# A recurrent layer with FP4 products on one core: the convolution over both input halves at once, and later `down` products

## The reference

```
k  = real(sum over n of W[h,n] * exp(dt[h]*Lambda[n]*l)),  l < 128    # one filter of 128 taps per feature
s  = causal convolution of xn with k along the sequence + xn * D
q(v) = v rounded to FP4 (E2M1) with one scale per 16 values, as float
h  = silu(q(xn) @ q(w_gate).T) * (q(xn) @ q(w_up).T)                   # 704 wide
g  = silu(q(h) @ q(w_down).T)
out = x + s * g
```

## Time and profile before

| | us |
|---|---|
| median of three runs | 711.54 (710.3 to 713.05) |
| the profiled execution | 711.99 |
| its span | 710.2 |
| TensorE busy (products) | 550.3 (77%) |
| VectorE busy | 587.8 (83%) |
| ScalarE busy | 404.3 (57%) |
| GpSimd busy | 193.6 (27%) |
| granted TensorE clock, mean | 0.95 |

### The profile page before, as it was taken

How to read it: one execution, slowest core, us unless ns; L and a number is a source line. 1 busy time by engine, 2 the same in 40 slices (tenths; PEclk the granted TensorE clock), 3 DMA queues, 4 the chain that set the end, 5 groups by cost and what they waited for, 6 DMA issues and landing times.

```text
span 710.2 us, 13747 instructions
## 1 busy us (share of the span) xinstructions
PE 550.3 (77%) x4856; PEld 391.6 (55%) x4856; DVE 587.8 (83%) x698; ACT 404.3 (57%) x562; POOL 193.6 (27%) x293
## 2 busy tenths in 40 slices
PE   0000087666888889999999999999999976868896
PEld 0000055234555557777777767777777744545564
DVE  7999999696998887888777758777777795979797
ACT  7940586465877765555555555555555534545554
POOL 1339410321232221111110102222111166565330
PEclk9999996888999999999999999999999997999999
DMA  6930000001000114444444444444444169674314
GB/s 208 348 105 0 0 15 16 15 4 35 16 16 16 44 44 135 132 124 128 120 138 123 125 114 135 134 128 133 127 124 129 47 114 209 152 177 85 93 59 121
DMA packets 109218, 70.79 MB, mean 100 GB/s; under 512 B 9072, under 2 KB 108912, under 8 KB 109168
## 3 DMA queue, kind: packets, MB, share of 16 engines
q1 hardware_dynamic: 101776, 62.73, 30.0%
q0 software_dynamic: 7392, 7.34, 6.9%
HBM read 61.28 MB, written 8.78 MB: 99 GB/s over the span
## 4 chain that ended last, share of the span: by engine, by line
PE 51%; DVE 11%; issue 8%; POOL 5%; DMA 3%; ACT 3%; DVEq 0%; ACTq 0%; POOLq 0%
PE ps L1208 23%; PE ps L1226 7%; PE ps L1245 6%; PE ps L1241 6%; PE ps L1228 4%; PE ps L1217 4%; DMA gbuf<-L_attn_u 3%; DVE work L851 2%; DVE work L846 2%; DVE work L877 1%; POOL gbuf L511 1%; PE ps L1196 1%; DVE xh L769 1%; ACT work L628 1%; DVE sm L793 1%
## 5 line engine op out<-in xcount | busy, mean ns | idle before, releaser
L1208 PE MATMUL ps<-wgu,work 128*128 128x512 f16 (+1 forms) x1152 | 253.7, 377 | 24.7 <-DVE work L877 23.5
L1208 PEld LDWEIGHTS ps<-wgu,work 128*128 128x128 f16 x1152 | 113.6, 101 | 142.6 <-issue 37.7
L614 ACT ACTIVATE work<-ps,con 128x704 f32<-128x704 f32 x64 | 54.2, 848 | 127.5 <-PE ps L1208 127.5
L1226 PE MATMUL ps<-wdh,work 128*128 128x256 f16 x704 | 92.4, 282 | 27.2 <-ACT work L609 27.2
L877 DVE TENSOR_TENSOR work<-work,ps 128x704 f32<-128x704 f32 x64 | 56.6, 885 | 64.8 <-ACT work L614 64.7
L609 ACT COPY work<-ps 128x1408 f16<-128x1408 f16 x64 | 84.9, 1328 | 15.5 <-PE ps L1217 15.1
L1226 PEld LDWEIGHTS ps<-wdh,work 128*128 128x128 f16 x704 | 68.5, 101 | 44.0 <-ACT work L609 32.1
L1245 PE MATMUL ps<-xh,work 128*128 x768 | 91.9, 239 | 0.0
L1241 PE MATMUL ps<-xh,work 128*128 x768 | 91.3, 238 | 0.0
L846 DVE SCALAR_TENSOR_TENSOR work<-work 128x960 f32<-128x960 bf16 (+2 forms) x67 | 71.9, 1112 | 23.3 <-ACT work L628 23.3
L511 POOL TENSOR_TENSOR gbuf<-gbuf,xh 128x512 f32<-128x512 f32 x28 | 39.9, 1450 | 126.8 <-DVE work L859 110.6
(11 more groups left out here) (152 smaller groups left out, 755.6 us busy)
## 6 DMA issues: line engine op xcount, KB each, us to landing
work<-kpad SPq DMA_DIRECT2D x64, 512.0 KB, 4.4
gbuf<-u_rev SPq DMA_DIRECT2D x4, 2048.0 KB, 18.3
work<-L_attn_u SPq DMA_DIRECT2D x32, 256.0 KB, 4.3
gbuf<-L_attn_u POOLq DMA_DIRECT2D x14, 512.0 KB, 5.9
out<-gbuf SPq DMA_DIRECT2D x14, 512.0 KB, 4.2
work<-L_attn_u SPq DMA_DIRECT2D x2, 512.0 KB, 3.7
work<-L_ffn_w_down SPq DMA_DIRECT2D x1, 704.0 KB, 7.1
work<-L_ffn_w_gate SPq DMA_DIRECT2D x1, 640.0 KB, 4.5
```

What stands on the lines that cost most here:

```text
L1208: last = T.matmul(p_gu[:, a:b], xT[par][:, t, c, :], wgu[:, part, c % 2, a:b], start=(n == 0), stop=(n == len(todo) - 1))
L1226: T.matmul(dst, hT[t][:, c, :], wdh[:, c, :], start=(c == 0), stop=False)
```

## The change

- The convolution takes both parts of `xh` as one operand of 128 columns (high tiles, then low tiles), with the template's high and low part: two products of 128 columns and two of 112 for each channel, four where there were six. (Low by low is now computed too.) The sums of the two halves come out apart: a bank holds 4 channels x 128, so a call of `conv` fills it, and each call waits for the evacuation of the one before.
- `y_copy` takes the high half to `yv` and the low half to a new buffer `ylo`, 256 values each, four calls a step; GpSimd adds them (`y_sum`, 512 values per partition, twice a step). `gated` and the tail wait for these sums (`y_p`) and not for the copies.
- The room for `ylo` is from `xhl`, which has one buffer where it had two; `x_parts` waits for the last transpose (`x_tp`). At the start `x_parts(1)` stands behind the weights. The final input `fin[1]` uses a template buffer.
- The `down` of a pair's second tile, its `silu_out` with it, moves to the next step, behind the first h transpose. `down` waits for the `silu_out` of the tile before it and no longer for the one before that.
- The four calls of `conv` are spread over TensorE's step; ScalarE's squares are split, and in the conv steps the first stands ahead of `silu_gate` and `x_norm` behind the second `h_copy`.
- GpSimd's `gated` products in steps 17 to 23 are one a step, ahead of the wait for x parts, where they were two in steps 16 to 23 behind it. From step 24 on there are up to three a step as before.
- TensorE's steps are written out without loops, ScalarE's steps 8 to 23 too.

```diff
-        xhl_words = carve(4 * H)
-        xhl = [xhl_words[:, 2 * H * i:2 * H * (i + 1)].bitcast(F16).rearrange("p (t c) -> p t c", t=2) for i in range(2)]
+        xhl = carve(2 * H).bitcast(F16).rearrange("p (t c) -> p t c", t=2)
+        ylo_words = carve(4 * H)
+        ylo = ylo_words.rearrange("p (j t c) -> p j t c", j=4, c=C4)
-        p_cv = ps[:, 3072:3584].rearrange("p (c t) -> p c t", c=G8)
+        p_cv = ps[:, 3072:3584].rearrange("p (c t) -> p c t", c=C4)
...
+            def y_sum(c8):
+                pool.wait_ge(cv_e, c8 * 2 + 2)
+                y8 = yv[:, 2 * c8:2 * c8 + 2].rearrange("p q t c -> p (q t c)")
+                lo = ylo[:, c8 % 2 * 2:c8 % 2 * 2 + 2].rearrange("p j t c -> p (j t c)")
+                nc.gpsimd.tensor_tensor(y8, y8, lo, ALU.add).then_inc(y_p, 1)
...
             for it in range(NP):
                 tables(it, it < NP - 2, it >= 1)
+                if S_CONV + 8 < it < S_OUT:
+                    some_gated(it, 1)
                 if it < NP - 2:
                     pool.wait_ge(x_hl, 2 * (it + 3))
...
+                if S_CONV <= it < S_OUT:
+                    for k in range(2):
+                        y_sum((it - S_CONV) * 2 + k)
+                if it >= S_OUT:
+                    some_gated(it, 3)
...
-            def y_copy(c8):
-                act.wait_ge(cv_h, c8 * 2 + 2)
-                nc.scalar.activation(yv[:, bass.ds(c8 * 2, 2), :, :],
-                                     p_cv.rearrange("p (a c) t -> p a t c", a=2), ACT.Copy,
+            def y_copy(q, k):
+                j = q * 4 + k
+                act.wait_ge(cv_h, j + 1)
+                y4 = yv[:, bass.ds(j, 1), :, :].rearrange("p q t c -> p c (q t)")
+                nc.scalar.activation(y4, p_cv[:, :, 0:NT], ACT.Copy, scale=con[:, C_CONV:C_CONV + 1])
+                after(act, y_p, q * 2 + k // 2 - 1)
+                nc.scalar.activation(ylo[:, k].rearrange("p t c -> p c t"), p_cv[:, :, NT:2 * NT], ACT.Copy,
                                      scale=con[:, C_CONV:C_CONV + 1]).then_inc(cv_e, 1)
-            def step(it, par, x, xt, xn, gu, ch, td, a2=False, cv=False):
+            def step(it, par, x, xt, xn, gu, ch, td, a2=False, cv=False, td1=True):
                 if td:
                     h_copy(it * 2 - 4, 0)
+                    if td1:
+                        if a2:
+                            after(act, a_lv, it - 2)
+                            after(act, a_lp, it - 2)
+                        silu_out(it * 2 - 5, 1, 1 - par)
                 if a2:
                     a_scale(it * 2)
+                if cv:
+                    y_copy(it - S_CONV, 0)
+                    square(it, 1 - par, x, ch, 0)
                 if gu:
                     silu_gate(it * 2)
+                if not cv:
+                    square(it, 1 - par, x, ch, 0)
                 if xt:
                     x_copy(it + 1, 1 - par)
-                square(it, 1 - par, x, ch)
+                if ch:
+                    square(it, 1 - par, x, ch, 1)
+                if cv:
+                    y_copy(it - S_CONV, 1)
...
                     silu_out(it * 2 - 4, 0, par)
-                if cv:
-                    y_copy(it * 2 - 2 * S_CONV)
                 if td:
                     h_copy(it * 2 - 3, 1)
+                if cv:
+                    y_copy(it - S_CONV, 2)
+                    x_norm(it + 3, 1 - par)
...
                     silu_gate(it * 2 + 1)
-                if td:
-                    silu_out(it * 2 - 3, 1, par)
                 if cv:
-                    y_copy(it * 2 - 2 * S_CONV + 1)
+                    y_copy(it - S_CONV, 3)
...
             def x_parts(p, par):
                 dve.wait_ge(x_r, p + 1)
-                after(dve, x_tp, p - 1)
+                after(dve, x_tp, p)
...
-                    after(pe, g_a, n - 1)
+                    after(pe, g_a, n)
...
-            def conv(c8, half):
+            def conv(j):
+                pe.wait_ge(t_in[j % 2], j // 2 * 16 + 16)
+                after(pe, cv_e, j)
+                for c in range(C4):
+                    col = xh[:, j, :, :, c].rearrange("p a t -> p (a t)")
+                    before = col.rearrange("p (s b) -> p s b", b=BPS)[:, :, 0:BPS - 1]
+                    dst = p_cv[:, c, :]
                     dst1 = dst.rearrange("p (s b) -> p s b", b=BPS)[:, :, 1:BPS]
+                    for part in range(2):
+                        T.matmul(dst, tpl[j % 2][:, 2 * c + part, 0:P], col, start=(part == 0), stop=False)
+                    for part in range(2):
+                        last = T.matmul(dst1, tpl[j % 2][:, 2 * c + part, P:2 * P], before, start=False, stop=(part == 1))
                 last.then_inc(cv_h, 1)
             def step(it, par, x, gu, td, cv=False):
+                j = (it - S_CONV) * 4
                 if td:
                     pe.wait_ge(hl_v, it - 1)
                     h_transpose(it * 2 - 4, 0, par)
+                    if it > 2:
+                        down(it * 2 - 5, 1)
+                if cv:
+                    pe.wait_ge(a_lv, NT // 8)
+                    pe.wait_ge(a_lp, NT // 8)
+                    conv(j)
                 if gu:
                     gate_up(it * 2, 0, par, it + 1)
                 if x:
                     x_transpose(it + 1, 1 - par)
+                if cv:
+                    conv(j + 1)
                 if td:
                     down(it * 2 - 4, 0)
+                    h_transpose(it * 2 - 3, 1, par, copied=it + 2 if x else None)
                 if cv:
-                    ...
+                    conv(j + 2)
                 if gu:
                     gate_up(it * 2 + 1, 1, par, None)
-                if td:
-                    down(it * 2 - 3, 1)
                 if cv:
-                    ...
+                    conv(j + 3)
+            for it in range(NP - 1):
+                step(it, it % 2, True, True, it >= 2, S_CONV <= it < S_OUT)
```

More of the change, by code:

```diff
@@ L507, in gated @@
                 pool.wait_ge(g_a, n * 4 + 4)
-                pool.wait_ge(cv_e, H // G8 // 2 * (half + 1))
+                pool.wait_ge(y_p, H // G8 // 2 * (half + 1))
                 gc = by_four(gbuf[:, 4 * n:4 * n + 4, :])[:, :, q0:q0 + HALF_Q, :]
@@ L551, in _, with some_gated @@
             todo = [(n, half) for half in range(2) for n in range(FIRST)]
-            made = 0
+            made = [0]
+            def some_gated(it, most):
+                ready = [
+                    (n, half) for n, half in todo
+                    if 4 * n + 3 <= it * 2 - 5 and (half == 0 or it >= S_OUT) and (half == 0 or (n, 0) not in todo)]
+                for n, half in sorted(ready, key=lambda job: (-job[1], job[0]))[0:most]:
+                    gated(n, half)
+                    todo.remove((n, half))
+                    made[0] += 1
+                    if half:
+                        add_input(n, n % 2, made[0])
             for it in range(NP):
                 tables(it, it < NP - 2, it >= 1)
+                if S_CONV + 8 < it < S_OUT:
+                    some_gated(it, 1)
                 if it < NP - 2:
@@ L561, in _ @@
                     a_low(it * 2)
[L562 to L575, removed]
+                if S_CONV <= it < S_OUT:
[3 more added lines that the diff above has]
+                    some_gated(it, 3)
+            some_gated(NP, 2 * FIRST)
+            some_gated(NP, 2 * FIRST)
         @block.scalar
@@ L620, in silu_out, with square @@
                                      scale=gsc[par][:, t:t + 1]).then_inc(g_a, 1)
[L622 to L629, removed]
+            def square(it, pp, x, ch, n):
+                if n == 0:
+                    after(act, hl_v, it - 1)
+                    after(act, x_hl, it * 2 + 4 if x else 2 * NP)
+                c = pieces(x, ch)[n]
+                act.wait_ge(v_v, pieces_before(it) + (n + 1))
+                nc.scalar.activation(d_bf[:, c], by_blk[pp][:, c], ACT.Square,
+                                     scale=float(SQ ** 0.5)).then_inc(sq_a, 1)
             def down_scale(p, par):
@@ L713, in _ @@
                 a_scale(2 * n + 1)
-            square(-2, 1, True, False)
+            square(-2, 1, True, False, 0)
             for m in range(2):
@@ L732, in _ @@
             weights_out(1, 8)
-            square(-1, 0, True, False)
+            square(-1, 0, True, False, 0)
             weights_out(9, 13)
@@ L739, in _ @@
             for it in range(PEEL):
-                step(it, it % 2, True, True, True, True, it >= 1, it >= 2, a2=True)
+                step(it, it % 2, True, True, True, True, it >= 1, it >= 2, a2=True, td1=it >= 3)
             with act.Fori(0, (S_CONV - PEEL) // 2) as q:
@@ L744, in _ @@
             act.wait_ge(con_ok, 1)
-            with act.Fori(0, (S_OUT - S_CONV) // 2) as q:
-                for par in range(2):
-                    step(q * 2 + (S_CONV + par), par, True, True, True, True, True, True, cv=True)
+            for it in range(S_CONV, S_OUT):
```

(4 more changed lines are left out.)

46 lines of the change are left out of this document (8 added, 38 removed).

## The result

| | before | after |
|---|---|---|
| median, 4 runs each | 711.84 (710.3 to 713.05) | 729.13 (726.86 to 729.72) |
| span of the profiled execution | 710.2 | 727.1 |
| granted clock, mean | 0.95 | 0.965 |

The ratio is 1.0238 [1.0208, 1.0268]. The prediction said 683 in a range of 675 to 708. Of its rivals (a), reading by column, came nearest, to which it had given 0.13 and the times 724 and 742.

A forecast was written before the change was run, and what follows sets the result against it. TensorE's work was taken to bound the 16 convolution steps. Products -29.3, jump -4.6, gated products +1, late down +3 and one xhl buffer +0.8 sum to -29.1 us, from a median of 711.54 to 683, range 675 to 708.

The forecast's parts named there:

- (a): Convolution products: strided operand read slowly column by column, 102 to 120 ns a product; 724 to 742 us; chance 0.13.
- The bound: Convolution steps 8 to 23: TensorE's work sets the step, 18.28 us before, and still does after at 16.25.
- The products: TensorE's convolution: 64 products of 58.5 ns replace 96 of 60; step 18.28 to 16.45 us, -29.3 us in all.
- (b): Convolution products: fixed 60 ns plus 0.42 ns per added column, 85 ns, step 18.0 us, 707 us; chance 0.08.
- the parts outside the conv steps: Gated products moved later +1, late down +3, one xhl buffer +0.8: together +4.8 us.
- ScalarE's copies: Convolution evacuation: eight copies of 0.47 us a step, +2.4 us on ScalarE, busy 12.5, no bound by itself.
- VectorE's turn: Convolution steps: VectorE needs 15.9 us, 0.5 less than TensorE's step, and allows no step under that.
- GpSimd's sums: Convolution steps: two sums a step on GpSimd cost 0, bounds 0 and 1.4 us a step.
- rival (c): Convolution steps: a GpSimd sum or gated product adds 1.4 us to VectorE's turn, step 17.3, 696 us; chance 0.13.
- The jump: TensorE's loop jump after step 15: its stall and half clock go with straight code, -4.6 us, bounds 0 and -4.6.
- Late `down`: Steps outside the convolution: second tile's down ahead of gate/up delays it in three steps, +3 us, bounds 0 and +9.
- The one xhl buffer: Start of the kernel: x parts of pair 1 move behind the weights, +0.8 us, bounds 0 and 1.5.

The follow-up runs named there:

- e3: Kernel before, convolution products reading 64 adjacent values instead of every fourth (values wrong, instructions the same): 669.69 us, ratio 0.9415.
- e9: Changed kernel with xh stored in pairs of channels instead of fours, everything computed: 668.02 us, ratio 0.9396 to the kernel before.
- e10: Kernel before with xh in pairs of channels and TensorE's steps written out without loops: 661.0 us, ratio 0.9282.
- e11: e10 plus ScalarE's squares in the changed order (first square, copy of xT, second square): 657.5 us, ratio 0.9252 to the kernel before.
- e1: Kernel before with 18 series of 32 products added at its end, varying columns and distance between them: 27 to 232 ns a product.
- e4: Changed kernel with xh laid out by single channel, so a channel's columns are adjacent, everything computed: 760.88 us, ratio 1.0711.
- e2: Changed kernel, convolution products reading 128 adjacent values instead of every fourth (values wrong, instructions the same): 670.89 us, ratio 0.9443.
- e5: Kernel before with TensorE's steps written out without loops, nothing else: 705.3 us against 710.62, ratio 0.991.
- e6: Kernel before with the second tile's down and its silu_out moved to the next step, nothing else: 715.84 us, ratio 1.0067.
- e7: Kernel before with xh stored in pairs of channels instead of fours, nothing else, everything computed: 671.32 us, ratio 0.9445.

## Why the prediction was wrong, by its steps

- **The bound** was right: TensorE set the conv step before and sets it after, and in e3, e9, e10 and e11.
- **The products, the step that failed.** "That 56 and 64 columns cost the same speaks for a fixed price of the pair (weight load and product), not one by column, so I take the middle of 56 and 60". (That middle is 58, not 58.5: 0.5 us in all.) The equality had another cause: both read 32 pieces of 16 bytes (e1: 60 with gaps, 53 without). A product of 64 adjacent values costs 29 ns, so there was no fixed price of 60. The 58.5 ns were 117, and the term -29.3 was +27. The bounds, 56 to 120, held it; the choice within them did not, and the range of the time left the upper one out.
- In the trace before stood a row against the choice: the transposes took 56 ns for 128 columns, so a pair of 64 columns at 60 could not be a fixed price of pairs as such. The prediction used that row for rival (a) ("slower than the transposes though they have half the columns") and against (b), but not against itself.
- The Trainium skill (SBUF — State Buffer, Door 1: The DMA port swizzle) has two hits per 16-byte line as enough for full bandwidth. TensorE's reads here disagree: two values to a line run at half the rate (116 for 56), four are needed. The 16 bytes themselves agree (232 against 228 once each value has its own). And of its 81 ns for a pair of 128 columns (TensorE: Matmul & The Clock Gate, Back-to-back issue gap) e1 shows 56.
- **Rival (a)** had the right place and, with 120 ns, the right price, but not the right reason: no price by column gives 112 columns what 128 cost, which is the objection that the prediction itself made with 56 and 64. Its 742 was 13 us too high: 3 for 120 instead of 117, the rest mostly because the parts outside the conv steps, +4.8 in the sum, came to -6.6. It had more in the trace for it than 0.13.
- **ScalarE's copies**: 0.47 us expected, 0.73 and 0.70 measured, since L618 writes in a row and L660 at a distance (e4 and e9: 475). No time came of it in the change, TensorE being later; in e2, where products are short, one call of `conv` a step waits for such a copy (TensorE starts at 363.00, the copy ends at 362.86), and e2's step is 16.37 where e9's is 16.15.
- **VectorE's turn**: 15.9 expected as the next bound. It is shorter: e10's steps take 15.36 us and hold 0.92 of waiting on VectorE. No run shows it as the bound of a conv step.
- **GpSimd's sums**: taken as 0, right here and in e9, where L830 has its 282 ns back. In the change they hold L830 up by 0.3 us a step, which VectorE had to spare; whether rival (c) would have come at a step of 16.45 us is not shown there, but in e9's 16.15 it did not.
- **The jump**: -4.6, measured -5.3 in all (e5, which takes TensorE's other loops out, too) and -4.6 in the step with the jump, and no "issue" stall in the conv steps after.
- **Late `down`**: +3, measured +5.2 alone (e6). In the change it came with the order of the squares; what the two do to the steps before step 8 (-4.7 us) the prediction did not have. The one xhl buffer is in the same part and was not tried alone.
- **Had the products cost 57 ns**, e9 shows the rest of the working: step 16.15 (16.45 said) and 668 us (683 said), the 15 us between them being mostly the gains outside the conv steps.

## What to carry to other kernels

Before merging products for fewer instructions, work out what each reads: columns, and 16-byte pieces of the moving operand at 1.8 ns each in these runs; here fewer instructions meant a third more of both. Two shapes at one price do not prove a fixed price: look for what else they share, and hold it against a third row (the transposes here). Change a layout halfway if its writers suffer: pairs cost them 4 to 8% more than fours, and gave TensorE all of the speed.

## What the runs showed of the hardware

- A product's distance to the next was, in every series and within 3 ns, the larger of its columns (128 in 56 ns, 64 in 29 at full clock) and 1.8 ns for each 16 bytes that its moving operand touches.
- The second price does not follow TensorE's clock. e1's last series (L1317, 256 values at distance 4, from 756.22) keeps 228 ns through the change of the clock, and 128 values at distance 8 have 228 at half clock, where 128 adjacent ones have 107. Windows of e1, columns as in the earlier trace rows:

```profile
756.30:758.00 1.70, 1.70 (x11) 0.91 (x9) 0.00 (x0) 0.00 (x0) 0.00 (x0) 0.50 0.00 0
758.40:762.00 3.60, 3.60 (x18) 1.83 (x16) 0.00 (x0) 0.00 (x0) 0.00 (x0) 1.00 0.00 0
```

- Writers with single 2-byte values far apart (e4): 4.9 us on ScalarE, 4.7 on VectorE, 4.8 on GpSimd, for what takes 1.05, 1.2 and 2.4 in fours (the change), and 1.09, 1.32 and 2.44 in pairs (e9).
- The loop's jump back on TensorE, with 8 steps written out per turn: 2.83 us of standing and a half clock behind it, a step 4.6 us longer than its neighbours; with shorter steps (e7) 4.75 us of standing and a step 7.3 us longer.
